# A decoder kernel: the products of queries with shifted keys, for batches two to four, on GpSimd in place of VectorE

## The reference, cut to what matters

```python
q = hidden_states @ Wq.T + bq
k = hidden_states @ Wk.T + bk
v = hidden_states @ Wv.T + bv
...
scores = jnp.einsum('bhqd,bhkd->bhqk', q, k) * SCALE
mask = neighborhood_mask(S)          # |j - i| <= 3
scores = jnp.where(mask[None, None], scores, -jnp.inf)
attn = jax.nn.softmax(scores, axis=-1)
```

## Time and profile before

| | us |
|---|---|
| three runs | 651.42, 651.47, 649.82 |
| median | 651.42 |
| span of the profiled execution, first to last instruction | 649.3 |
| busy: TensorE / VectorE / ScalarE / GpSimd | 592.1 / 462.0 / 413.9 / 110.2 |

### The profile page before, as it was taken

The page is one execution under the profiler, slowest core; times in us unless marked ns, Lnnn a source line. Parts: engine busy times, 40 slices in busy tenths (PEclk is TensorE's granted clock), DMA queues, the critical chain, the costliest instruction groups (busy, mean ns, idle before and its releaser), DMA issues.

```text
span 649.3 us, 10805 instructions
## 1 busy us (share of the span) xinstructions
PE 592.1 (91%) x3516; PEld 383.1 (59%) x3516; DVE 462.0 (71%) x1396; ACT 413.9 (64%) x807; POOL 110.2 (17%) x118
## 2 busy tenths in 40 slices
PE   3579997879999999999989999699999999999995
PEld 1162252326556464655555766466768887888885
DVE  3746756644486637887958889978659996996744
ACT  2108998968688988689979554354564356445541
POOL 1000002320011422100362103511013111001200
PEclk9587999989999999999999999899999999999999
DMA  8931000120001130000130001400010000000000
GB/s 273 407 152 38 2 1 0 55 77 10 5 18 55 37 89 21 14 14 13 39 108 9 17 18 41 109 17 14 21 27 25 2 17 2 1 0 18 1 18 18
DMA packets 28183, 29.26 MB, mean 45 GB/s; under 512 B 4953, under 2 KB 24289, under 8 KB 27745
## 3 DMA queue, kind: packets, MB, share of 16 engines
q1 hardware_dynamic: 26080, 24.36, 11.3%
q0 software_dynamic: 2048, 4.20, 2.3%
HBM read 19.51 MB, written 9.04 MB: 44 GB/s over the span
## 4 chain that ended last, share of the span: by engine, by line
PE 68%; issue 6%; ACT 3%; DVE 3%; POOL 1%; DMA 1%; POOLq 0%; SPq 0%; DVEq 0%; ACTq 0%
PE bank L887 16%; PE bank L903 8%; PE bank L805 8%; PE bank L1044 7%; PE bank L894 4%; PE bank L984 2%; PE bank L961 2%; PE bank L776 2%; PE bank L699 2%; PE bank L700 2%; PE bank L701 2%; PE bank L879 1%; PE bank L977 1%; POOL x_rows L1754 1%; PE bank L858 1%
## 5 line engine op out<-in xcount | busy, mean ns | idle before, releaser
L1122 ACT ACTIVATE a_big<-feat,txt_cols 128x512 f32<-128x512 f32 x270 | 173.7, 713 | 4.6 <-PE bank L805 4.3
L887 PE MATMUL bank<-gup_sb,x_cols 128*128 x240 | 126.5, 614 | 0.5 <-ACT x_cols L1163 0.4
L805 PE MATMUL bank<-a_big,score_pad 128*32 128x512 f32 x616 | 102.7, 614 | 3.2 <-ACT a_big L1122 3.1
L1237 ACT ACTIVATE a_big<-bank,cols_sb 128x512 f32<-128x512 f32 x72 | 49.2, 687 | 56.7 <-PE bank L701 55.8
L903 PEld LDWEIGHTS bank<-down_sb,hid_sb 128*128 128x128 f32 x480 | 62.3, 191 | 31.9 <-issue 31.9
L1527 DVE SCALAR_TENSOR_TENSOR gated_sb<-gated_sb,bank 128x256 f32<-128x256 f32 x120 | 50.0, 417 | 42.4 <-ACT gated_sb L1188 41.7
L1044 PEld LDWEIGHTS bank<-rw_sb,a_big 128*128 128x128 f32 x576 | 69.4, 192 | 2.8
L1044 PE MATMUL bank<-rw_sb,a_big 128*128 128x128 f32 x576 | 69.9, 275 | 0.0
L903 PE MATMUL bank<-down_sb,hid_sb 128*128 x480 | 64.0, 276 | 2.7 <-ACT hid_sb L1170 2.6
L1188 ACT ACTIVATE gated_sb<-bank 128x256 f32<-128x256 f32 x120 | 45.8, 382 | 30.8 <-PE bank L887 30.0
L1529 DVE SCALAR_TENSOR_TENSOR gated_sb<-gated_sb,bank 128x256 f32<-128x256 f32 x120 | 50.5, 421 | 4.1
(11 more groups left out here) (279 smaller groups left out, 952.4 us busy)
## 6 DMA issues: line engine op xcount, KB each, us to landing
gup_sb<-gup SPq DMA_DIRECT2D x1, 4096.0 KB, 15.7
y_rows<-x_tiles SPq DMA_DIRECT2D x60, 64.0 KB, 1.5
down_sb<-down SPq DMA_DIRECT2D x1, 2048.0 KB, 17.4
x_rows<-b_y SPq DMA_DIRECT2D x2, 960.0 KB, 10.4
x_tiles<-x_rows SPq DMA_DIRECT2D x4, 448.0 KB
rw_sb<-rw SPq DMA_DIRECT2D x1, 1152.0 KB, 19.7
a_qT<-x_T SPq DMA_DIRECT2D x4, 256.0 KB, 2.7
a_tok<-x_tok SPq DMA_DIRECT2D x4, 256.0 KB, 3.0
```

The costliest lines, as they stand in the source:

```text
L805: last = mm(P[2][32 * j:32 * j + 32, :], score_pad[:, 31 - i:63 - i], ring[k % RING], start=(i == 0), stop=(KCOL * (i + 1) + j >= KEYS))
L887: mm(P[3 + h][:, :], x_col[i % 2], part[:, bass.ds(at_of[i], I0)], start=True, stop=True)\
L1122: act(ring[(k + j) % RING], feat[b][:, :], ACT.Tanh, bias=txt_cols[:, c:c + 1])\
L1237: act(hid6[u % 2][:, c * S:(c + 1) * S], P[5 + n % 2][:, :], ACT.Gelu, bias=col("rb1", n))\
```

## The change

`product` on VectorE returns at once for batches 1 to 3. GpSimd gets a step `product` that issues the same 7 multiplications for these batches, in the place that the list gives the step, with one more wait: for the blend of the batch before (`attn0_psum`), the last reader of `b_big`.

```diff
@@ -1315,6 +1315,8 @@
             def product(b, i):
+                if b >= 1:
+                    return
                 eng.wait_ge(qkv_ready, 3 * b + 2)
                 for o in range(2 * i, min(2 * i + 2, OFFS)):
                     tt(prod[b][o], a_q, a_k[:, o:o + S], ALU.mult).then_inc(prod_ready, 1)
@@ -1709,6 +1711,16 @@
+            def product(b, i):
+
+                if b == 0:
+                    return
+                if i == 0:
+                    eng.wait_ge(attn0_psum, b)
+                eng.wait_ge(qkv_ready, 3 * b + 2)
+                for o in range(2 * i, min(2 * i + 2, OFFS)):
+                    tt(prod[b][o], a_q, a_k[:, o:o + S], ALU.mult).then_inc(prod_ready, 1)
```

More of the change, by code:

```diff
@@ L1768, in gather @@
                         .then_inc(picked_in[t], 16)
-            steps = {"input": attended_input, "norm_a": norm_a, "norm_b": norm_b, "pow": gate_powers, "sum": sums,
+            steps = {"input": attended_input, "product": product, "norm_a": norm_a, "norm_b": norm_b, "pow": gate_powers, "sum": sums,
                      "residual": residual, "scatter": scatter, "gather": gather}
```

## The result

The changed kernel takes **670.62 us** (median of 4 runs, 667.77 to 673.15) against 651.01 us before (649.82 to 651.47, 4 runs beside it): ratio 1.0298, 95% interval 1.0264 to 1.0331. That is 19.6 us more. The forecast was 668.1 us, 16.7 more, with a range of 662 to 675. In a later comparison, with six runs, the same kernel took 669.02 us (1.0252, 1.0224 to 1.0281), 17.1 us more than the kernel before beside it. The two intervals overlap; the forecast is nearer to the second.

The account below looks back on a forecast made before the run. TensorE was taken to bound the kernel, with GpSimd's scatters holding up its first tile. Terms of 2.2 + 11.2 + 3.0 + 0.3 = 16.7 us on the 651.42 us median gave 668.1 us, range 662 to 675.

Parts of the forecast that it names:

- The mechanism: Whole kernel: TensorE bounds it, batch 0's scatters delay its first tile, and delays shift the rest rigidly; 16.7 us in all.
- batch 1: From 60.22 us: GpSimd's products end later, so TensorE's scores and next rho round, and the waiting tanh, come late: +2.2 us.
- batch 2: Products ahead of batch 0's scatters on GpSimd wait for `a_k` and delay TensorE's first tile: +11.2 us.
- batch 3: From 212.83 us: late products stall the full TensorE, so `to_tokens` comes late: +3.0 us.
- The price of a product: One multiplication on GpSimd: 1.28 us, taken from its additions, so 8.97 us for seven; bounds 1.01 and 1.96 us.
- The wait for the first sum: In batch 1: GpSimd's products were let begin only after VectorE's first sum, 0.4 us late.
- The held sums: In batch 1: GpSimd's products and VectorE's two sums meet and hold each other up; second sum might wait 1.28 us.
- the rival by which GpSimd keeps the ports: In batch 1: gapless products never let VectorE's second sum in between; 6.6 us more, 674.7 us; chance 0.12.
- The clock: TensorE's half-speed stretch after the longer stall ahead of the first tile lasts a little longer: +0.3 us.
- a term put at nothing: Behind batch 3's products: GpSimd's bias row moves to some 231 us, covered by the first gather's wait: no cost.
- The signs of being wrong: Wrong: product under 1.1 or over 1.5 us, sum held several products, new half-clock beyond 4 us, lag shrinks after 240 us.
- Not slower: Rival at the first tile: later idle time of TensorE takes up the scatters' delay; 650.4 us; chance 0.02.

Follow-up runs that it names:

- dummy2: Kernel before, with GpSimd also making batch 2's seven products into unread memory while VectorE still makes the real ones: 664.37 us, ratio 1.0219.
- double2: Changed kernel, with GpSimd making each product of batch 2 once more into unread memory: 676.47 us, ratio 1.0400.
- scatfirst: Changed kernel, with all products of batch 2 put behind the eight scatters of batch 0 on GpSimd: 665.63 us, ratio 1.0205.
- only1: Kernel before, with only the products of batch 1 moved to GpSimd: 654.74 us, ratio 1.0035.
- only2: Kernel before, with only the products of batch 2 moved to GpSimd: 662.20 us, ratio 1.0163.
- only3: Kernel before, with only the products of batch 3 moved to GpSimd: 655.39 us, ratio 1.0051.
- shifted_k: Changed kernel, with the keys stored one column (4 bytes) further on in SBUF: 668.7 us in one run.
- only1_late: As only1, but GpSimd waits for VectorE's two sums before it begins its products: 654.53 us, ratio 1.0027 against the kernel before.
- split13: Kernel before, with only offsets 5 and 6 of batches 1 and 3 moved to GpSimd: 653.08 us, ratio 0.9999.

## Why the forecast came out right, point by point

**The mechanism.** TensorE bounds the kernel, GpSimd is free only in the mean, and the scatters of batch 0 stand behind the products: shown by `dummy2` (they alone delay the tile), `double2` (one for one) and `scatfirst` (the other order makes `score` late). That each delay shifts the rest of the program rigidly: the delays stay the same over hundreds of us in the table, and the three single kernels add up within the noise.

**The terms of the sum.** In us, as read in the traces:

| term | forecast | changed kernel, first and second profile | alone |
|---|---|---|---|
| batch 1 | 2.2 | 1.7 and 1.8 | 1.7 (only1) |
| batch 2 | 11.2 | 12.5 and 12.4 | 10.8 (only2) |
| batch 3 | 3.0 | 3.8 and 3.6 | 3.8 (only3) |
| the rest behind 122 us (clock; scatters of 1.50 us in only1 and only3) | 0.3 | 2.3 and -0.2 | 1.8, -0.1, 1.9 |
| a wait at 209 us | 0 | 0.9 and 0 | none |

**The price of a product** was mis-sized: 1.28 us, by the additions, against a mean of 1.19 with some overlap between neighbours; seven took 7.95 to 8.3 us instead of 8.97. That is 0.7 to 1.0 less work per batch. Of it 0.5 shows in batch 1 (1.7 for 2.2), 0.7 in batch 2 (10.5 for 11.2 at the first tile of `only2`), and 0.9 in batch 3, where `to_tokens` of the second profile has moved by 2.1 us since 205 us, for 3.0. The wait for the first sum, 0.4 us in the working, did not come about either: both engines began within 0.03 us, and the sum was held.

**The held sums** were seen as possible and not counted. The longest sum took 1.528 us where the median is 0.480; before, the maximum was 0.977. This is the group by line of the kernel after:

```profile
L1371 DVE TENSOR_SCALAR a_big<-feat,txt_cols x38: 473/480/1528, 51.6 to 364.4; 128x512 f32<-128x512 f32 x38
```

Each of the two was held by about one product (2.76 us for both, 0.88 before), not for all seven. That refutes the rival by which GpSimd keeps the ports, 674.7 us: products that follow each other without a gap do let a waiting sum in between. The rule of the Trainium skill (page "SBUF — State Buffer", section "Who interferes with whom"), by which whoever begins first holds the shared pair for its whole instruction and the other is blocked, agrees with the length of the hold. That section of the Trainium skill counts among what takes the shared pair both multiplications with two inputs in SBUF, as in `dummy2`, and operations like these sums, with one, if they run in a mode that uses two ports; whether they do, no run shows. That the waiting engine comes next, ahead of an instruction already queued on the other, is what these traces of batches 1 and 2 add. In batch 3 one row goes the other way, below.

**The clock** is the first of two terms that were too small, and hid the error of the price. Windows of the kernel after (columns as the earlier trace rows), the first two at places where the clock was at 1.00 before; the third around 432 us; the last is that third place in the second profile of the same kernel.

```profile
124.00:130.00 6.00, 5.75 (x26) 2.24 (x18) 3.23 (x19) 4.70 (x10) 0.00 (x0) 0.72 0.00 0
238.00:239.00 1.00, 1.00 (x12) 0.28 (x8) 0.00 (x0) 0.60 (x1) 0.69 (x2) 0.50 0.19 66
432.00:443.00 11.00, 8.86 (x28) 6.02 (x29) 10.72 (x27) 2.64 (x7) 7.25 (x8) 0.53 0.49 134
```
```profile
432.00:443.00 11.00, 9.19 (x43) 5.88 (x44) 10.59 (x28) 4.48 (x10) 5.90 (x7) 0.85 0.39 104
```

In batch 2 a stretch of 3.4 us at 125 us, in both profiles, made `a_k` 1.6 us late; with it, 12.5 is 10.9 and 1.6, and `only2`, which has no such stretch, has 10.8. The stretch behind the stall ahead of the first tile grew from 3.4 us to 20.5, but TensorE waits for half of it, and behind the first tile it cost only 0.3 to 0.6, where 0.3 was forecast. At 432 us the first profile had 10.2 us at half clock and the second 3.4, as before: 2.3 us between two executions of one program. The Trainium skill (page "TensorE: Matmul & The Clock Gate", section "Part 1: The HAM clock gate (the "warmup" mystery)") has these two levels too, 1.2 and 2.4 GHz, and says that the point of change moves by half a microsecond from run to run; the stretches at 432 us differ by 6.8 us in length, which is more.

**Batch 3, and a term put at nothing.** Behind the wait of 2.18 us the first profile ran at half clock for 3.4 us, while TensorE was full, and `to_tokens` came 1.7 us later for it. The prediction had named such a stretch as possible ("2 us at half speed lose 1 us each") and left it to the range. But the second profile has the same wait and no such stretch, and its batch 3 costs 3.6 us all the same. Its lines: VectorE's last multiplication of the softmax of batch 3, GpSimd's bias row, the transpose on TensorE that waits for the softmax (`to_rows`), and a window from the products to there.

```profile
244.01 2.49 DVE L1341 TENSOR_TENSOR a_s<-a_s,a_den 128x512 f32<-128x512 f32 x1
244.66 1.28 POOL L1711 TENSOR_TENSOR a_tok<-a_tok,rows_sb 128x512 f32<-128x512 f32 x1
246.56 0.66 PE L756 MATMUL bank<-const_sb,a_s 128*128 128x128 f32 x4 [1.25 <-DVE a_s L1341]
228.00:246.00 18.00, 14.78 (x94) 6.29 (x93) 8.43 (x12) 15.87 (x31) 14.62 (x14) 1.00 0.09 29
```

The same multiplication before, and in the first profile of the kernel after:

```profile
227.27 0.69 DVE L1339 TENSOR_TENSOR a_s<-a_s,a_den 128x512 f32<-128x512 f32 x1
```
```profile
247.13 0.81 DVE L1341 TENSOR_TENSOR a_s<-a_s,a_den 128x512 f32<-128x512 f32 x1
```

Before, the bias row was done at 222.50, 4.8 us ahead of this multiplication. The products push six scatters and the row back, and in the second profile the row falls on it: 2.49 us instead of 0.69, and TensorE waits 1.25 us where it waited for nothing. The multiplication began 0.65 us ahead of the row, beside the last scatter, and still ended 0.56 behind it. Where the clock was at half, the whole softmax came 1.7 us later and only brushed the row (0.81). So it is in all six traces with this batch on GpSimd: either the half clock (first profile, `only3`, `scatfirst`) or the held multiplication (second profile, `double2`, `shifted_k`, 2.48 to 2.50 us), and from the first half of `score` to behind `to_rows` TensorE loses 3.3 us in the first three and 3.1 in the others. No kernel moves the bias row alone, so this is read from traces and not tested. The prediction had seen the row move to some 231 us and counted only the first gather as what it could delay; what VectorE does beside it was put at nothing.

So the sum held by errors of opposite sign. In the second profile: 2.0 us too much for the products (0.4, 0.7 and 0.9 in the three batches), and 3.1 too little, 1.6 for the clock in batch 2 and 1.5 for the held multiplication in batch 3. The mechanism was right; that the number came within 0.4 us in one comparison and 2.9 in the other is in part luck.

**The signs of being wrong.** By the prediction's own list two of them came. Products took under 1.1 us: 1.08 to 1.10 for four offsets of seven. And the clock stayed at half for more than 4 us where it had been at full: the stretch from 135.6 us lasts 20.5 us, where before it had 3.4, and in the first profile the one at 432 us lasts 10.2. Neither changed the mechanism, and the others did not come: no sum lay still for several products, and the distance between the two kernels does not shrink behind 240 us by more than 0.3. The first scatter came 7.1 us after `a_k` and not some 10; six products of 1.28 would have made 7.7, so that figure did not follow from the working.

**Not slower**, 650.4 us: refuted by every kernel that moves a whole batch.

**What stays open.** Why the stretches at 108 and 125 us are there. Every kernel in which batch 1 was late had an extra stretch at half clock that began between 69 and 127 us (both profiles of after, `only1`, `only1_late`, `scatfirst`, `double2`, `shifted_k`, `split13`), and none of the others (both of before, `only2`, `only3`, `dummy2`). But the one at 125, which costs, was only in the two of after, `shifted_k` and `split13`, and TensorE was all but full there. The same stretch of work in `only1` and in `only2`, where it comes 2.86 us earlier:

```profile
107.00:112.00 5.00, 3.98 (x13) 1.18 (x14) 2.98 (x13) 4.97 (x9) 1.64 (x1) 0.66 0.00 0
```
```profile
104.14:109.14 5.00, 3.98 (x13) 0.97 (x14) 2.98 (x13) 4.97 (x9) 1.64 (x1) 1.00 0.00 0
```

TensorE is busy for 3.98 us of 5 in both, and in `only1` alone the clock is halved. Nor is it known why the wait of 2.18 us in batch 3 is followed by half clock in three traces and not in three others, why the stretch at 432 us lasts three times as long in one execution, why two scatters took 1.50 us in `only1` and `only3` and none over 1.23 before, or what brought 0.9 us around 209 us in the first profile (a wait of TensorE that no trace of the other kernels has).

No version beat the kernel before; `split13` is level with it.

## What to carry to other kernels

A busy share says nothing of who is free at a given moment: GpSimd was at 17%, and still, in the traces, each microsecond put ahead of its eight scatters came out at the end. Before work is moved to an idle engine, read what stands behind it on that engine's list, above all DMAs that it issues, and read what VectorE does with operands in SBUF at that moment, for then the two take turns. Ask the same of everything that stands behind the moved work and slips with it: here a bias row of 1.28 us, harmless where it was, fell on a multiplication of VectorE. And where a move brings a new wait of TensorE of some 2 us at a place where it is full, a stretch at half clock can follow: here it did in three traces of six, for 3.4 us, and `to_tokens` behind it came 1.7 us later.

## What was new of the hardware

- A multiplication over 128x512 with both inputs in SBUF took GpSimd 1.08 to 1.11 or 1.26 to 1.29 us, by the address of the shifted operand (`shifted_k`); VectorE took 0.68 to 0.74 for all offsets.
- Multiplications with two inputs on both engines at once alternate: VectorE's took 1.46 us in the mean and GpSimd's 1.60, instead of 0.63 and 1.15 (`dummy2`).
- VectorE's sum with one input in SBUF, 0.48 us, was held beside GpSimd to 1.53 us at most, each by one product and no longer.
- VectorE's multiplication with two inputs in SBUF, 0.69 us, took 2.49 when it began beside a scatter and 0.65 us ahead of an addition of GpSimd: the addition went first (second profile of after, `double2`, `shifted_k`).
- Scatters issued by GpSimd while VectorE multiplied took up to 1.50 us instead of 0.96. In `only1`, where VectorE makes the products of batch 2, two of the eight did, and two in `only3` and about as long in `split13`:

```profile
130.13 1.50 POOL L1766 DMA_INDIRECT x_rows<-a_x,slots  x1 [0.30 <-issue]
131.93 1.50 POOL L1766 DMA_INDIRECT x_rows<-a_x,slots  x1 [0.30 <-issue]
```
